# The first FFN product of a cross-attention block as seven block products instead of eight, with W1's parts streamed

## The chip, the cores and the metric

The kernel runs on one core of a Trainium2 chip. The metric is the device time of one execution in microseconds (us), lower is better.

## The reference

The input x has 8 batches of 1024 tokens with 512 channels, the context 8 times 64 rows of 384 channels. All is float32.

```python
x = x + xattn(layernorm(x), ctx_768, Wq, bq, Wk, bk, Wv, bv, Wo, bo)   # 16 heads of 32, 64 keys, softmax
h = layernorm(x) @ W1 + b1                                            # 512 -> 2048
imag = w_imag * sin(theta + 0.1 * h)
q = h + (cos(theta) * w_real + sin(theta) * w_imag) * imag * 0.1
x = x + relu(q) @ W2 + b2                                             # 2048 -> 512
```

The sine, the gate and the relu are elementwise on the hidden values h, of which there are 8192 x 2048.

## The kernel before

**Precision.** Each float32 product is made of three matmuls of 128x128 weights against 128x512 moving columns in the fp32r type: both operands are split into a high and a low part, and high x high, high x low and low x high are added up in PSUM (`product`, lines 1394 to 1396). The low part is the operand less its high part. So every operand of a product costs ScalarE (ACT) a copy to the high part and VectorE (DVE) or GpSimd (POOL) a subtraction for the low part.

**Stage A, attention.** 8192 tokens are 16 tiles of 512 (`TILES`), a tile has 4 blocks of 128 rows (`NB`), and 4 groups of heads make 64 steps. TensorE does queries, scores, transposes, values and output projection. Its result, x1, goes to DRAM (`x1_dram`). From the third tile on, the layer-normed rows are turned from token-major to channel-major without TensorE: DVE turns 32x32 squares (`turn_rows`), SyncE (SP) sends them to DRAM in four DMAs a half tile (`carry_out`) and reads them back in another order (`carry_back`).

**Stage B, FFN.** For each tile t and each chunk f of 128 of the 2048 hidden channels, TensorE makes the hidden values by 4 products of 3 matmuls (`xt_hi`/`xt_lo` against `w1a`/`w1b`), and then the second product of an earlier chunk, `second(j - LAG_B)`, 4 blocks of 3 matmuls. One chunk is 24 matmuls. W1 and W2 stay in SBUF in high and low parts. The other engines do, for each chunk: ACT `turns` (line 1010, from PSUM) and `hid` (1012, from PSUM); DVE `frac`, the rounding (1350); POOL turns less the rounding (820); ACT the sine (995); DVE `wave`, hid plus gain times sine (1320); ACT the relu to `act_hi` (1001); DVE `act_lo` (1325). For each tile there are also: POOL adds of the bias bo (637) and b2 (645), statistics (1049), the normalised rows (865), the turn of the rows through DRAM, and at the end DVE's addition of the four blocks of the second product (`residual`, 1313) and the store. Four hidden banks of PSUM rotate; `second` holds the other four for a whole tile.

Every engine runs its queue in the order written. Waits are on counting semaphores. SP issues nearly all DMAs, and it too waits in order.

**Between the stages.** At step 63 of stage A, SP loads x1 of tiles 0 and 1 (557, 558). Tile 0 is biased, normalised and turned by 16 transposes on TensorE (1400), right behind the last output projections. The first 8 chunks of W1 were split during stage A, one per tile (`split_hi`, `split_lo`).

## Time and profile before

| | us |
|---|---|
| median of three timed executions (2029.12 to 2029.51) | 2029.39 |
| span of the profiled execution (first to last instruction) | 2027.3 |
| first FFN matmul starts, us from the span's start | 630.33 |
| last matmul starts | 2023.53 |
| busy in the span: PE / DVE / ACT / POOL | 2014.9 / 1342.4 / 1131.6 / 1021.5 |

The profiled execution is one execution, and its own time is its span; a timed execution counts 2.1 us more. A busy PE says only that matmuls are in flight: a matmul is shown as 389 ns long while a new one starts about every 227 ns, so the pace is read from counts in a window. PEclk is the granted TensorE clock as a share of full speed; it reads 1.00 all through both stages.

### The profile page before, as it was taken

What the parts mean: (1) busy time and instruction counts of PE and PEld (TensorE: products, weight loads), DVE (VectorE), ACT (ScalarE), POOL (GpSimd) and SP (SyncE); (2) the same over time, 40 slices, a digit from 0 to 9 for tenths busy, and PEclk for the clock granted to TensorE, in tenths of its full rate; (3) what the DMA queues carried; (4) which work ended last, traced back from release to release, by engine and by line L of the source; (5) the groups of instructions that cost most, each with busy time, mean ns of one, the idle gap of its engine ahead of it and who ended that gap; (6) DMA issues with size and microseconds to landing.
All of it is one profiled execution on the core that took longest, in us unless ns stands there. A gap on an engine that the chain in (4) does not pass through costs nothing.

```text
span 2027.3 us, 26664 instructions
## 1 busy us (share of the span) xinstructions
PE 2014.9 (99%) x9498; PEld 1684.9 (83%) x9498; DVE 1342.4 (66%) x1983; ACT 1131.6 (56%) x1979; POOL 1021.5 (50%) x708
## 2 busy tenths in 40 slices
PE   9999999999999999999999999999999999999999
PEld 7788888888888888888888888888888888888887
DVE  8988888888876665655555555565655555555554
ACT  6767767667665655544554454545545454554453
POOL 6877777777774453435334343433435334343521
PEclk9999999999999999999999999999999999999999
DMA  7565675655524311121111212211130211112100
GB/s 240 150 164 136 169 175 138 173 137 164 143 66 144 107 42 42 45 81 27 57 42 42 54 40 73 42 42 42 42 83 21 64 43 42 46 48 73 42 22 21
DMA packets 232822, 168.51 MB, mean 83 GB/s; under 512 B 154353, under 2 KB 184049, under 8 KB 232689
## 3 DMA queue, kind: packets, MB, share of 16 engines
q1 hardware_dynamic: 231824, 166.76, 29.8%
q8 instruction: 75, 1.23, 0.3%
q14 instruction: 59, 0.48, 0.1%
q10 hardware_dynamic: 864, 0.04, 0.0%
HBM read 98.34 MB, written 68.16 MB: 82 GB/s over the span
## 4 chain that ended last, share of the span: by engine, by line
PE 91%; DVE 4%; ACT 2%; POOL 1%; issue 1%; DMA 1%; SPq 0%; ACTq 0%; DVEq 0%; POOLq 0%
PE psum L1394 29%; PE psum L1396 29%; PE psum L1395 29%; PE psum L1487 2%; DVE hid L1320 1%; POOL prob L679 0%; DVE act_lo L1325 0%; POOL prob L700 0%; ACT act_hi L1001 0%; ACT hid L1012 0%; DVE top L1177 0%; DVE prob L1168 0%; DMA x_sb<-in_x 0%; DVE xt_lo L1067 0%; DVE xt_lo L1277 0%
## 5 line engine op out<-in xcount | busy, mean ns | idle before, releaser
L820 POOL TENSOR_TENSOR frac<-turns,frac 128x512 f32<-128x512 f32 x256 | 333.3, 1302 | 826.9 <-DVE frac L1350 826.9
L1320 DVE SCALAR_TENSOR_TENSOR hid<-frac,gain,hid 128x512 f32<-128x512 f32 x256 | 321.7, 1257 | 144.2 <-ACT frac L995 143.1
L1394 PE MATMUL psum<-w_hi,act_hi 128*128 128x512 f32 x1024 | 398.3, 389 | 0.0
L1395 PE MATMUL psum<-w_lo,act_hi 128*128 128x512 f32 x1024 | 398.3, 389 | 0.0
L1396 PE MATMUL psum<-w_hi,act_lo 128*128 128x512 f32 x1024 | 398.3, 389 | 0.0
L1010 ACT ACTIVATE turns<-psum,u_shift 128x512 f32<-128x512 f32 x256 | 176.5, 689 | 328.4 <-PE psum L1396 271.2
L1001 ACT ACTIVATE act_hi<-hid 128x512 fp32r<-128x512 f32 x256 | 161.8, 632 | 353.9 <-DVE hid L1320 353.9
L1325 DVE SCALAR_TENSOR_TENSOR act_lo<-hid,act_hi 128x512 fp32r<-128x512 f32 x256 | 197.6, 772 | 178.1 <-ACT act_hi L1001 178.1
L1350 DVE TENSOR_SCALAR frac<-turns 128x512 f32<-128x512 f32 x256 | 111.4, 435 | 248.1 <-ACT turns L1010 248.1
L1395 PEld LDWEIGHTS psum<-w_lo,act_hi 128*128 128x128 f32 x1024 | 192.3, 188 | 40.0
L1394 PEld LDWEIGHTS psum<-w_hi,act_hi 128*128 128x128 f32 x1024 | 192.1, 188 | 39.9
L1396 PEld LDWEIGHTS psum<-w_hi,act_lo 128*128 128x128 f32 x1024 | 192.1, 188 | 39.8
L1394 PE MATMUL psum<-xt_hi,w1a_hi 128*128 128x512 f32 x512 | 199.5, 390 | 0.5 <-DVE xt_lo L1067 0.3
L1396 PE MATMUL psum<-xt_hi,w1a_lo 128*128 128x512 f32 x512 | 199.2, 389 | 0.0
L1395 PE MATMUL psum<-xt_lo,w1a_hi 128*128 128x512 f32 x512 | 199.2, 389 | 0.0
L1396 PE MATMUL psum<-xt_hi,w1b_lo 128*128 128x512 f32 x512 | 199.2, 389 | 0.0
L1394 PE MATMUL psum<-xt_hi,w1b_hi 128*128 128x512 f32 x512 | 199.2, 389 | 0.0
L1395 PE MATMUL psum<-xt_lo,w1b_hi 128*128 128x512 f32 x512 | 199.2, 389 | 0.0
L1012 ACT ACTIVATE hid<-psum,par 128x512 f32<-128x512 f32 x256 | 174.5, 682 | 0.0
L995 ACT ACTIVATE frac<-frac 128x512 f32<-128x512 f32 x256 | 161.4, 630 | 0.0
L700 POOL TENSOR_TENSOR prob<-prob,top 128x1024 f32<-128x1024 f32 x64 | 122.1, 1907 | 73.2 <-DVE top L1177 73.1
L679 POOL TENSOR_TENSOR prob<-prob,inv 128x1024 f32<-128x1024 f32 x64 | 123.6, 1931 | 42.1 <-DVE inv L1159 42.0
(149 smaller groups left out, 4013.1 us busy)
## 6 DMA issues: line engine op xcount, KB each, us to landing
res<-in_x SPq DMA_DIRECT2D x64, 256.0 KB, 3.8
x_dram<-res SPq DMA_DIRECT2D x64, 256.0 KB, 3.1
x_sb<-in_x SPq DMA_DIRECT2D x15, 1024.0 KB, 6.4
x_sb<-x_dram SPq DMA_DIRECT2D x15, 1024.0 KB, 5.5
xn<-turn_dram SPq DMA_DIRECT2D x30, 512.0 KB, 5.1
out<-x_sb SPq DMA_DIRECT2D x15, 1024.0 KB, 4.4
turn_dram<-kt SPq DMA_DIRECT2D x112, 128.0 KB, 2.4
x_sb<-turn_dram SPq DMA_DIRECT2D x28, 512.0 KB, 6.3
```

The costliest lines, as they stand in the source:

```text
L679: pool.tensor_tensor(rows, rows, inv[:, (i - 1) % 2, :].unsqueeze(2) .to_broadcast([P, NB * HG, KEYS]), ALU.mult).then_inc(prob_done, 1)
L700: pool.tensor_tensor(rows, rows, top[:, i % 2, :].unsqueeze(2).to_broadcast([P, NB * HG, KEYS]), ALU.subtract).then_inc(shift_done, 1)
L820: pool.tensor_tensor(frac[:, j % 2, :], turns[:, j % 2, :], frac[:, j % 2, :], ALU.subtract)\
L995: act.activation(frac[:, j % 2, :], frac[:, j % 2, :], ACT.Sin, scale=SIN_SCALE).then_inc(sin_done, 1)
L1001: act.activation(act_hi[:, j % ACTS, :], hid[:, j % 2, :], ACT.Relu).then_inc(act_hi_done, 1)
L1010: act.activation(turns[:, j % 2, :], hidden, ACT.Identity, bias=u_shift[:, f:f + 1], scale=0.1 / TWO_PI).then_inc(turns_done, 1)
L1012: act.activation(hid[:, j % 2, :], hidden, ACT.Identity, bias=par[:, 3, f:f + 1])\
L1320: dve.scalar_tensor_tensor(out=hid[:, j % 2, :], in0=frac[:, j % 2, :], scalar=gain[:, f:f + 1], in1=hid[:, j % 2, :], op0=ALU.mult, op1=A ...
L1325: dve.scalar_tensor_tensor(out=act_lo[:, j % ACTS, :], in0=hid[:, j % 2, :], scalar=0.0, in1=act_hi[:, j % ACTS, :].bitcast(F32), op0=ALU. ...
L1394: pe.matmul(o, a_hi, b_hi, start=first, stop=False)
L1395: pe.matmul(o, a_hi, b_lo, start=False, stop=False)
L1396: return pe.matmul(o, a_lo, b_hi, start=False, stop=last)
```

## The change

Two token tiles (512 tokens each) and two hidden chunks (128 channels each) form a 2x2 product, with the 512 input channels cut into two halves of 256. It is made by Strassen's scheme in Winograd's form: seven products of block sums where eight block products would do. The eight pairs of tiles (`FFN_PAIRS`) each run 8 steps p of two chunks. A step has seven products P1 to P7 of 6 matmuls each.

- **TensorE.** In the sweep over p it runs P1, P6, P4, P2, P5, P7, then (from p = 1) `second` of the two chunks of step p-1 for the pair's first tile, then P3. P2 is accumulated on top of P1 in bank 0, P7 on P6 in bank 1, P3 on P5 in bank 2, and P4 is alone in bank 3. After P1, a copy of it is taken (`keep_p1`) before P2 may start; after P6, `sum_u` before P7; after P5, `sum_v`, `hidden_21` and `hidden_22` before P3. After step 7 come the last two chunks of the first tile, and then a second sweep: `second` of all 16 chunks for the pair's second tile, whose hidden values wait in `late_hid`.
- **Operands of the pair.** Both tiles are turned through DRAM (also the first two; the 16 transposes at the start of stage B are gone), POOL makes four sums (`operand_sums`), and ACT and DVE make high and low parts of seven operands of 128x1024 (`operand_hi`, `operand_lo`).
- **W1.** During stage A, 28 jobs make the seven parts of W1 (POOL sums, ACT high parts, low parts on POOL and DVE in turn) and store them in DRAM. In stage B each product's part (256 KB) is loaded into a ring of 8.
- **W2.** It is split in the first pair's sweep (ACT and POOL), stored in DRAM, and then loaded for each chunk and tile (512 KB) into a ring of 4.
- **Hidden values.** In each step ACT adds a copy of P1, and DVE adds five sums with PSUM; `hid` from PSUM on ACT is left for one of the four blocks. Output sums go to a buffer of their own, `acc`, loaded from x1.
- **Bias.** POOL adds bo to tiles 2T+2 and 2T+3 in steps 0 and 1 of pair T, and the last bias to the two tiles of `acc` in steps 2 and 4, each as two instructions of 128x1024, ahead of the step's `fraction`s. The first two tiles' bo is added in stage A.

```diff
+PRODUCTS = ("P1", "P6", "P4", "P2", "P5", "P7", "P3")
+NP = len(PRODUCTS)
+OPERANDS = ("B11", "B21", "B22", "T1", "T2", "T4", "T3")
+MOVING = {"P1": "B11", "P2": "B21", "P3": "B22", "P4": "T4", "P5": "T1", "P6": "T2", "P7": "T3"}
+BANK_OF = {"P1": 0, "P2": 0, "P6": 1, "P7": 1, "P5": 2, "P3": 2, "P4": 3}
...
+        xo_hi = sbuf(pb, "xo_hi", [P, NP, 2, TOK], F32R)
+        xo_lo = sbuf(pb, "xo_lo", [P, NP, 2, TOK], F32R)
+        w1_ring = sbuf(pb, "w1_ring", [P, W1_SLOTS, 2, 2 * P], F32R)
+        temps = sbuf(pb, "temps", [P, 2, 2 * TOK])
+        p1_sb = sbuf(pb, "p1_sb", [P, TOK])
...
+        late_hid = sbuf(pb, "late_hid", [P, FC, TOK])
+        w2_ring = sbuf(pb, "w2_ring", [P, W2_SLOTS, 2, C], F32R)
+        acc = sbuf(pb, "acc", [P, 2, NB, C])
...
+        def events(T):
+            order = []
+            for p in range(FP):
+                i = T * FP + p
+                order += [("product", i, name) for name in PRODUCTS[:-1]]
+                if p:
+                    order += [("second", first_half(T, 2 * p - 2), None), ("second", first_half(T, 2 * p - 1), None)]
+                order.append(("product", i, PRODUCTS[-1]))
+            order += [("second", first_half(T, FC - 2), None), ("second", first_half(T, FC - 1), None)]
+            return order + [("second", second_half(T, c), None) for c in range(FC)]
         block = stack.enter_context(nc.Block())
...
+            def load_w1(n):
+                if n >= W1_SLOTS:
+                    sp.wait_ge(prod, n - W1_SLOTS + 1)
+                pair, m = divmod(n % (NP * FP), NP)
+                sp.dma_start(w1_ring[:, n % W1_SLOTS].bitcast(F32).rearrange("p s x -> p (s x)"), w1s[pair, m])\
+                    .then_inc(w1_in[n % W1_SLOTS], 16)
...
+            def load_w2(e):
+                c = e % FC
+                sp.wait_ge(f_psum, e - W2_SLOTS + 1)
+                sp.wait_ge(w2_stored[c % W2_SLOTS], 16 * (W1_JOBS // W1_OUTS + c // W2_SLOTS + 1))
+                sp.dma_start(w2_ring[:, e % W2_SLOTS].bitcast(F32).rearrange("p s x -> p (s x)"), w2s[c])\
+                    .then_inc(w2_in[e % W2_SLOTS], 16)
...
+            sp.wait_ge(q_psum, GROUPS)
+            for slot in range(W1_OUTS):
+                sp.wait_ge(w1_stored[slot], 16 * len(range(slot, W1_JOBS, W1_OUTS)))
+            for n in range(W1_SLOTS):
+                load_w1(n)
+            for c in range(STAGE):
+                load_w2_raw(c)
+            rows_back(1)
...
+                        for p, s, half in ((5, 0, 0), (6, 0, 1), (7, 1, 0)):
+                            if more and at == first_half(T, 2 * p - 1):
+                                rows_out(2 * T + 2 + s, half)
+                        if more and at == second_half(T, 1):
+                            rows_out(2 * T + 3, 1)
+                        if at == second_half(T, 1):
+                            store_acc(2 * T)
+                        if more and at == second_half(T, 3):
+                            rows_back(2 * T + 3)
+                            load_acc(2 * T + 2)
+                        if T + 2 < FFN_PAIRS and at == second_half(T, FC - 2):
+                            for s in range(2):
+                                load_rows(2 * T + 4 + s)
...
+                    if more and p < 2:
+                        for half in range(2):
+                            add_row_bias(2 * T + 2 + p, half)
...
+                    if p in (2, 4):
+                        for half in range(2):
+                            add_last_bias(2 * T + p // 4, half)
+                    for kind in range(3):
+                        fraction(4 * i + kind)
...
+                fraction(4 * (T * FP + FP) - 1)
+                if more:
+                    operand_sums(T + 1, ("T1", "T2", "T4", "T3"))
...
+            def keep_p1(i):
+                act.wait_ge(prod, at_prod(i, "P1"))
+                act.wait_ge(v_done, i)
+                act.activation(p1_sb[:], psum[:, BANK_OF["P1"], :], ACT.Copy).then_inc(p1_done, 1)
...
+            for T in range(FFN_PAIRS):
+                more = T + 1 < FFN_PAIRS
+                for p in range(FP):
+                    i = T * FP + p
+                    if p:
+                        sine(4 * i - 2)
+                        positive(first_half(T, 2 * p - 1))
+                        turn(i - 1, 3)
+                    keep_p1(i)
+                    if T == 0:
+                        w2_to_hi(2 * p)
+                        w2_to_hi(2 * p + 1)
+                    if p:
+                        sine(4 * i - 1)
+                    for at, s, half in ((4, 0, 0), (5, 0, 1), (6, 1, 0), (7, 1, 1)):
+                        if more and p == at:
+                            ffn_rows(2 * T + 2 + s, half)
+                    turn(i, 0)
+                    hidden(i)
+                    sine(4 * i)
+                    turn(i, 1)
+                    turn(i, 2)
+                    positive(first_half(T, 2 * p))
+                    sine(4 * i + 1)
...
+            def sum_u(i):
+                T, p = divmod(i, FP)
+                dve.wait_ge(prod, at_prod(i, "P6"))
+                dve.wait_ge(p1_done, i + 1)
+                if T:
+                    dve.wait_ge(act_lo_done, second_half(T - 1, 2 * p) + 1)
+                dve.scalar_tensor_tensor(out=late_hid[:, 2 * p, :], in0=psum[:, BANK_OF["P6"], :],
+                                         scalar=par[:, 3, 2 * p:2 * p + 1], in1=p1_sb[:], op0=ALU.add, op1=ALU.add)\
...
+            def hidden_22(i):
+                p = i % FP
+                dve.wait_ge(v_done, i + 1)
+                dve.wait_ge(c21_done, i + 1)
+                rows = late_hid[:, 2 * p + 1, :]
+                dve.tensor_tensor(rows, psum[:, BANK_OF["P5"], :], rows, ALU.add).then_inc(c22_done, 1)
...
+            for j in range(NP):
+                operand_lo(0, j)
+            dve.wait_ge(y_psum, TILES * NB)
+            dve.wait_ge(last_done, 1)
+            for T in range(FFN_PAIRS):
+                more = T + 1 < FFN_PAIRS
+                for p in range(FP):
+                    i = T * FP + p
+                    if p:
+                        wave(4 * i - 3)
+                        hidden_12(i - 1)
+                        whole(4 * i - 1)
+                        positive_lo(first_half(T, 2 * p - 1))
+                    sum_u(i)
+                    if p:
+                        wave(4 * i - 2)
+                        wave(4 * i - 1)
+                    whole(4 * i)
...
+                    if more and p == 7:
+                        turn_late_rows(2 * T + 3, 0)
+                    sum_v(i)
+                    hidden_21(i)
+                    hidden_22(i)
+                    wave(4 * i)
+                    whole(4 * i + 1)
+                    whole(4 * i + 2)
+                    positive_lo(first_half(T, 2 * p))
+                i = T * FP + FP
+                wave(4 * i - 3)
+                hidden_12(i - 1)
+                whole(4 * i - 1)
+                positive_lo(first_half(T, FC - 1))
+                wave(4 * i - 2)
+                positive_lo(second_half(T, 0))
+                add_outputs(2 * T)
+                positive_lo(second_half(T, 1))
+                wave(4 * i - 1)
+                if more:
+                    turn_late_rows(2 * T + 3, 1)
+                for c in range(FC):
+                    if c + 2 < FC:
+                        positive_lo(second_half(T, c + 2))
+                    if more and c in XT_AT:
...
+            def strassen(i, name):
+                p, n, j = i % FP, at_prod(i, name) - 1, OPERANDS.index(MOVING[name])
+                pe.wait_ge(w1_in[n % W1_SLOTS], 16 * (n // W1_SLOTS + 2))
+                if p == 0:
+                    pe.wait_ge(xo_lo_done, NP * (i // FP) + j + 1)
+                if name == "P1" and i:
+                    pe.wait_ge(hid_done, i)
+                elif name == "P6" and i:
+                    pe.wait_ge(v_done, i)
+                elif name == "P4" and i:
+                    pe.wait_ge(c21_done, i)
+                elif name == "P5" and i:
+                    pe.wait_ge(c12_done, i)
+                elif name == "P2":
+                    pe.wait_ge(p1_done, i + 1)
+                elif name == "P7":
+                    pe.wait_ge(u_done, i + 1)
+                elif name == "P3":
+                    pe.wait_ge(c22_done, i + 1)
+                w, to = w1_ring[:, n % W1_SLOTS], psum[:, BANK_OF[name], :]
+                for k in range(2):
+                    cols = slice(k * P, (k + 1) * P)
+                    m = product(to, (w[:, 0, cols], w[:, 1, cols]), (xo_hi[:, j, k, :], xo_lo[:, j, k, :]),
+                                name in OPENS and k == 0, k == 1, name not in OPENS)
+                m.then_inc(prod, 1)
...
-                    hi, lo = (w1a_hi, w1a_lo) if f < HALF1 else (w1b_hi, w1b_lo)
-                    for k in range(KC):
-                        if f == 0:
-                            pe.wait_ge(xt_lo_done, (TILES + t) * KC + k + 1)
-                        m = product(psum[:, f % NB, :], (hi[:, f % HALF1, k, :], lo[:, f % HALF1, k, :]),
-                                    (xt_hi[:, k, :], xt_lo[:, k, :]), k == 0, k == KC - 1)
-                    m.then_inc(h_psum, 1)
```

## Rows read from the trace of the kernel before

**Rows 1.** The page: busy time of each engine over the span

```profile
PE 2014.9 (99%) x9498; PEld 1684.9 (83%) x9498; DVE 1342.4 (66%) x1983; ACT 1131.6 (56%) x1979; POOL 1021.5 (50%) x708
```

**Rows 2.** Windows: stretch, length, busy us (count) of five engines, PEclk, DMA share, GB/s

```profile
500.00:600.00 100.00, 100.00 (x547) 86.54 (x547) 77.82 (x122) 65.30 (x126) 72.67 (x46) 1.00 0.43 115
1000.00:1500.00 500.00, 500.00 (x2208) 414.01 (x2207) 286.79 (x392) 251.29 (x415) 207.74 (x145) 1.00 0.18 47
```

**Rows 3.** Groups by line: busy us, mean ns | idle before, releaser

```profile
L820 POOL TENSOR_TENSOR frac<-turns,frac 128x512 f32<-128x512 f32 x256 | 333.3, 1302 | 826.9 <-DVE frac L1350 826.9
L1320 DVE SCALAR_TENSOR_TENSOR hid<-frac,gain,hid 128x512 f32<-128x512 f32 x256 | 321.7, 1257 | 144.2 <-ACT frac L995 143.1
L1325 DVE SCALAR_TENSOR_TENSOR act_lo<-hid,act_hi 128x512 fp32r<-128x512 f32 x256 | 197.6, 772 | 178.1 <-ACT act_hi L1001 178.1
L1010 ACT ACTIVATE turns<-psum,u_shift 128x512 f32<-128x512 f32 x256 | 176.5, 689 | 328.4 <-PE psum L1396 271.2 <-DVE act_lo L1325 56.6
L995 ACT ACTIVATE frac<-frac 128x512 f32<-128x512 f32 x256 | 161.4, 630 | 0.0
L679 POOL TENSOR_TENSOR prob<-prob,inv 128x1024 f32<-128x1024 f32 x64 | 123.6, 1931 | 42.1 <-DVE inv L1159 42.0
L1350 DVE TENSOR_SCALAR frac<-turns 128x512 f32<-128x512 f32 x256 | 111.4, 435 | 248.1 <-ACT turns L1010 248.1
...
L1313 DVE TENSOR_TENSOR x_sb<-psum,x_sb 128x512 f32<-128x512 f32 x64 | 39.9, 682 | 2.4 <-PE psum L1396 2.4
```

**Rows 4.** Timeline, four places: start us, length, engine, line

```profile
616.31 1.29 POOL L637 TENSOR_TENSOR x_sb<-x_sb,bo_row 128x512 f32<-128x512 f32 x1 [2.91 <-DMA x_sb<-x_dram]
...
676.63 0.74 DVE L1320 SCALAR_TENSOR_TENSOR hid<-frac,gain,hid 128x512 f32<-128x512 f32 x1
676.79 1.74 POOL L820 TENSOR_TENSOR frac<-turns,frac 128x512 f32<-128x512 f32 x1 [6.01 <-DVE frac L1350]
...
1511.69 1.28 POOL L820 TENSOR_TENSOR frac<-turns,frac 128x512 f32<-128x512 f32 x1 [4.74 <-DVE frac L1350]
1511.70 1.83 DVE L1320 SCALAR_TENSOR_TENSOR hid<-frac,gain,hid 128x512 f32<-128x512 f32 x1
```

**Rows 5.** DMA issues: count, KB each, median us from issue to landing

```profile
out<-x_sb SPq DMA_DIRECT2D x15, 1024.0 KB, 4.4
turn_dram<-kt SPq DMA_DIRECT2D x112, 128.0 KB, 2.4
x_sb<-turn_dram SPq DMA_DIRECT2D x28, 512.0 KB, 6.3
```

**Rows 6.** Windows: a turned tile read back, and an x1 tile loaded; last two columns

```profile
1486.00:1488.00 2.00, 2.00 (x11) 1.65 (x10) 1.21 (x2) 1.18 (x3) 1.29 (x1) 1.00 1.02 214
...
1518.00:1520.00 2.00, 2.00 (x10) 1.65 (x10) 0.79 (x2) 1.03 (x2) 0.00 (x0) 1.00 1.04 404
```

**Rows 7.** Timeline of the passage from stage A to stage B

```profile
615.51 0.43 SPq L558 DMA_DIRECT2D x_sb<-x_dram  x1
...
620.64 2.47 DVE L1049 BATCH_NORM_STATS2 stats<-x_sb 128x6 f32<-128x512 f32 x4
...
623.81 1.02 POOL L616 TENSOR_TENSOR rstd<-var_eps,minus_half 128x4 f32<-128x4 f32 x1 [2.06 <-DVE var_eps L1056]
...
625.06 2.93 ACT L865 ACTIVATE xn<-x_sb,shift_rows,rstd 128x512 f32<-128x512 f32 x4 [5.58 <-DVE shift_rows L1061]
...
627.70 0.39 PE L1396 MATMUL psum<-wo_hi,o_lo 128*128 128x512 f32 x1
...
630.33 0.47 PE L1394 MATMUL psum<-xt_hi,w1a_hi 128*128 128x512 f32 x1 [0.26 <-DVE xt_lo L1067]
```

**Rows 8.** TensorE at the start, a turn of squares, and the last matmul

```profile
3.03 8.90 PE L1436 MATMUL psum<-kbd 128*128 128x512 f32 x30 [3.03 <-DVE kbd L1094]
...
675.17 1.24 DVE L1379 STREAM_TRANSPOSE turned_early<-xn 128x1024 f32<-128x1024 f32 x1
...
2023.53 0.39 PE L1396 MATMUL psum<-w_hi,act_lo 128*128 128x512 f32 x1
```

895 lines of the change are left out of this document (549 added, 346 removed).

## The prediction

> **What bounds the kernel now.** I read the busy times of the page first: TensorE has work in flight for 2014.9 of 2027.3 us, no other engine for more than 1342.4 [rows 1]. Then the windows, for the pace. Stage B issues 2208 matmuls in 500 us, 226.5 ns each, at a granted clock of 1.00 (the upper level, 2.4 GHz) and with nothing between them. VectorE is busy 287, ScalarE 251 and GpSimd 208 of those 500 us [rows 2]. The groups by line say why those engines aren't busier: nearly all their idle time ends on one another, in a ring turns, rounding, fraction, sine, wave, relu, low part, and this ring starts when TensorE delivers a chunk [rows 3]. So time goes by the count of matmuls, and the question for the change is whether the ring still fits beside a shorter TensorE stream, and what happens where TensorE's stream is cut.
>
> **The matmuls taken out: -87.0 us.** Before, a pair of tiles and two chunks take 2 x 2 x 12 = 48 matmuls of the first product; after, 7 x 6 = 42. That is 6 x 64 = 384 fewer, x 0.2265 = 87.0 us. FFN matmuls go from 6144 (1391.6 us; measured 630.33 to 2023.76, that is 1393.4 [rows 7, 8]) to 5760, 1304.6 us. A step of the sweep becomes 66 matmuls, 14.95 us; step 0 has no `second` and is 9.5 us.
>
> **The passage between the stages: +37.5 us.** Before, the last output projection ends at 627.9 and the first FFN product starts at 630.3 [rows 7]. After, P6 needs operand T2, which needs both tiles turned through DRAM. I follow that chain on the clock of before.
> VectorE begins statistics at 620.6 and does both tiles (2 x 3.1), so the shift of tile 0 comes at 627.0 and that of tile 1 after its GpSimd step at 628.1. ScalarE normalises at 0.73 a block: 628.6, 630.1, 631.5, 633.0. VectorE turns the first two halves by 631.4 (1.24 each, [rows 8]).
> SP sends half 0 at 630.2 to 632.2 and half 1 by 634.2 (four issues; one takes 0.43 [rows 7], I count 0.5), they land 2.4 after issue, and SP reads them back at 634.6 and 636.1; landing takes 6.3 [rows 5], so 640.9 and 642.4. The same DRAM buffer then takes tile 1: out 640.9 to 644.9. Before it is read back, SP issues 8 loads of W1 parts and 2 of W2, some 0.4 us each: the read goes out at 649.5 and, behind 2.6 MB of loads, lands at about 658.
> GpSimd forms T1 and T2 (2 x 2.5, below), the high and low part take 1.2 each: P6 at about 667. T4's low part waits behind GpSimd's next sum, so P4 starts at 670.6, which in an undisturbed step is 2.7 us after its beginning. The step thus begins in effect at 667.9, against 630.3. Bounds: +25 (both round trips at the 5 us of an unqueued read, sums at 1.3) to +48.
> TensorE stands still for some 18 us twice here. At the start of the kernel, after a standstill, 30 matmuls of this size take 8.9 us, 297 ns each [rows 8], against 6.8 at the usual pace. I add that 2.1 us once. The trace's clock shows 1.00 there, so it does not say why. The Trainium skill (TensorE: Matmul & The Clock Gate, What's actually happening) says that an idle array falls to 1.2 GHz and is back at 2.4 GHz once it has been busy; no row of this trace shows a fall inside the run, and the sum goes by the row.
>
> **The wait before P3 of step 0: +18 us.** With no `second` before it, P3 waits for P7 through `sum_v`, `hidden_21`, `hidden_22`. P7 ends at 8.15, is visible 0.2 later, and three VectorE operations with PSUM, 0.68 each [rows 3], end at 10.4. 2.25 us in each of 8 pairs. In other steps the two `second` hide it (P3 starts at 13.6).
>
> **The ring in the sweep: +23 us.** Per step VectorE has 4 waves, 5 sums, 4 roundings, 2 low parts: in pure work 4 x 0.74 + 5 x 0.68 + 4 x 0.44 + 2 x 0.77 = 9.7 us [rows 3, 4], and 1.2 for statistics and turns (8 of 0.62 and 4 of 1.24 over 8 steps [rows 7, 8]). But a wave reads two SBUF tensors, and beside GpSimd's operation it is held: both started at 1511.7, GpSimd took 1.28, the wave 1.83 = 1.28 + 0.55; when the wave came first (676.63), GpSimd took 1.74 instead of 1.29 [rows 4]. So they go one at a time.
> The Trainium skill (SBUF — State Buffer, Who interferes with whom) says that the one that starts first keeps the port for its whole instruction. The rows show it for 1.3 us instructions only; by the rule the new ones of 128x1024 hold VectorE twice as long.
> A plain step by hand, from P1 = 0: P2 done 5.6, turns 6.3, rounding 6.8, fraction 8.2, sine 8.8; h21 and h22 9.7 and 10.4; wave 11.1; fractions 12.9 and 14.7; wave of the second chunk 15.25; `hidden_12` 15.9; relu and turns on ScalarE 16.7; `keep_p1` of the next step 17.35. P2 needs it at 14.95 + 4.08 = 19.0: 1.7 us to spare.
> With two bias instructions ahead of the step's first fraction the ring gets longer than the step. A block of 512 takes 1.29 undisturbed [rows 4], so 1024 takes 2.55; the row of that size, with one operand broadcast, is 1.93 [rows 3]. I take 2.2, and 0.45 each time VectorE's turn is let in: 5.3 us a step, a ring of some 15.9 against 14.95. At 1.93 it is 15.2, at 2.55 with every wave held 16.6. The spare 1.7 goes in the first such step. From step 0 (only 9.5 + 2.25 long) into step 1 TensorE waits 1.3 us before P2; into steps 2 and 3, 0.9 each; step 3 has no bias and recovers; step 4 just fits. 3.1 us x 7, and 1.3 in the last pair, which has fewer adds. Bounds 8 (1.93) and 40 (2.55).
> The first pair also splits W2: GpSimd 2 x 1.3 more a step, ScalarE 2 x 0.63. On a step with bias that adds about 2.6: +8 us (3 to 12).
>
> **The DMA queue in the second sweep: +17.5 us.** SP's transfers share one queue. When chunk 1 of that sweep is done (5.4 us in) SP issues a W2 part (0.52 MB), half a turned tile (0.52), the store of 1.05 MB (4.4 us when alone [rows 5]); then two W2 parts, the turned tile back (1.05), the load of acc (1.05) and a fourth W2 part, which chunk 8 needs at 21.8. At 404 GB/s, and 214 for the turned tile [rows 6], that is 5.2 + 1.3 + 2.6 + 2.6 us at 404, 4.9 for the tile read back, and, by my estimate from the slower of the two rates, 1.2 more for the half tile: 17.8 us of transfer. It starts at 6.7, since a transfer starts over 1 us after its issue, and lands at 25.2. TensorE waits 3.4 us if the queue is strictly in order, nothing if transfers overlap. I take 2.5, x 7 pairs.
>
> **The attention stage: +3 us.** GpSimd gets 14 low parts (2.2 each) and 16 sums (1.3), VectorE 14 low parts less 8 old ones. GpSimd is busy 72.7 and VectorE 77.8 of 100 us there [rows 2], and these stand at ends of steps; I take 3 of 0 to 10. W1's part loads (256 KB for each 1.36 us product, 193 GB/s against 404) come seven products ahead and stay hidden, as do W2's in the first sweep.
>
> **Sum.** -87.0 + 37.5 + 2.1 + 18 + 23 + 8 + 17.5 + 3 = +22.1. Span 2027.3 -> 2049.4; a timed run counts 2.1 more, so 2051.
>
> **Rivals.** (1) *Faster: the ring stays inside the step.* Place: GpSimd's bias adds in steps 0 to 2. If a 1024 add goes at the 1.93 of the attention rows or faster and the waves slip in between, the 23 shrinks to 2 and the first pair's 8 to 1: 2023. For it: such a row exists, and TensorE waits nowhere now. Against: the add of two real rows has 1.29 for 512. The point at which it decides: one-off costs are 37.5 + 2.1 + 8 + 3 = 50.6, so 36.4 us are left for 8 pairs, 4.55 each; P3's wait takes 2.25, so ring and DMA together must stay under 2.3 us a pair. I have 5.3. (2) *Slower still: the lock decides.* Adds of 2.55 that hold each wave to their end, DMA strictly in order: ring 40 and DMA 24, passage 42, first pair 12: 2083. (3) *The DMA queue costs nothing* because transfers overlap: 2033. For it: the load share reads above 1.00 at places; against: shares near 1.00 are full engines. (4) *The passage is much shorter*, 20 us instead of 37.5: 2033. Against: each round trip is three SP waits in order.
>
> **How the numbers follow.** Forecast, with every term near its middle, 0.42; rival 1 and what is like it 0.25, of which 0.02 ends within 0.2%; rival 2, 0.15; rivals 3 and 4, 0.18, of which 0.05 faster and 0.03 within 0.2%. A measurement of this kernel tells about 0.2% (4 us) from no change. Faster 0.28, same 0.05, slower 0.67. The likeliest case's own range is 2036 to 2066. The range for 8 in 10 takes in most of rivals 1 and 2: 2010 to 2078.
>
> **What would show it.** In the profile after: 9098 matmuls; first FFN matmul about 648, the second product only about 667; windows inside stage B where TensorE has 2208 a 500 us in plain steps; a wait of TensorE for VectorE's `hidden_22` of 2.2 us eight times; waits for ScalarE's `p1_sb` of about 1 us in steps 1 to 3 and none in 5 to 7; one wait for `w2_ring` of about 3 us in seven pairs. The forecast fails if the passage is much under 37 us, or if the waits for `p1_sb` and `w2_ring` are absent or are several us in every step.

## The result and the profile after

The changed kernel takes 2200.07 us (median of 4 runs, 2199.49 to 2202.72) against 2029.26 beside it (4 runs, 2029.07 to 2029.51): ratio 1.0845, 95% interval 1.0830 to 1.0861. I had forecast slower, 2051 with a range to 2078. The side was right, the size was not: 171 us in place of 22.

The page of the kernel after, busy time of each engine, beside [rows 1]; then the granted clock; then the windows of [rows 2]:

```profile
PE 1995.6 (91%) x9098; PEld 1628.4 (74%) x9098; DVE 1711.0 (78%) x2279; ACT 1095.1 (50%) x1855; POOL 1192.7 (54%) x728
```

```profile
core 0: 2197.5 us, clock 0.971
```

```profile
500.00:600.00 100.00, 95.92 (x517) 81.10 (x517) 84.27 (x131) 65.04 (x125) 77.72 (x51) 1.00 0.65 181
1000.00:1500.00 500.00, 460.11 (x1958) 371.40 (x1957) 383.48 (x463) 221.49 (x342) 221.52 (x121) 0.98 0.74 235
```

The 400 matmuls less are there (9098). But 500 us of stage B hold 1958 where 2208 stood, and the 100 us of the attention stage 517 where 547 stood. VectorE went from 287 to 383 of 500 us.

I split the difference of the spans, 170.2 us, at four places: the last output projection (it ends 0.23 us after its last start), P4 of the first pair (2.7 us behind the step's start in effect), the starts of the pairs, and the end. The matmuls of the first two places, by timeline:

```profile
672.36 0.39 PE L1805 MATMUL psum<-wo_hi,o_lo 128*128 128x512 f32 x1
...
717.47 0.76 PE L1803 MATMUL psum<-xo_hi,w_ring 128*128 128x512 f32 x1 [19.30 <-DVE xo_lo L1649]
718.03 0.63 PE L1804 MATMUL psum<-xo_lo,w_ring 128*128 128x512 f32 x1
...
720.77 0.76 PE L1803 MATMUL psum<-xo_hi,w_ring 128*128 128x512 f32 x1 [0.40 <-DVE xo_lo L1649]
```

Pairs are counted from 0, as steps are.

| part | forecast | measured |
|---|---|---|
| 384 matmuls | -87.0 | -87.0 |
| attention stage (last projection 627.9 -> 672.6) | +3 | +44.7 |
| passage, with its slow clock (720.77 - 2.7 - 672.6 - 2.4) | +39.6 | +43.0 |
| first pair from there, over its 163.1 us of matmuls | +15.9 | +35.5 |
| pairs 1 to 6 over theirs | +47.1 | +130.2 |
| pair 7 | +3.6 | +5.3 |
| stalls of stage B that before already had | | -1.8 |
| sum | +22 | +170 |

So 42 us of the error lie in the attention stage, 83 in pairs 1 to 6, 20 in the first pair. Pair 7, which prepares nothing for a next pair, is nearly as forecast. That is the first hint: what costs is not the seven products.

What TensorE waited for, over the whole span (us in total, times, longest). L1684 is `hidden_22`, for which P3 waits; `p_sb` is the copy of P1, for which P2 waits; then come the W2 ring and the two waits of the passage.

```profile
PE psum L1803 <- DVE late_hid L1684: 41.0, 26, 2.5
PE psum L1803 <- ACT p_sb L1272: 34.5, 29, 6.0
PE psum L1803 <- DMA w_ring<-w2s: 32.1, 9, 5.5
PE psum L1803 <- DMA w_ring<-w1s: 22.5, 1, 22.5
PE psum L1803 <- DVE xo_lo L1649: 19.7, 2, 19.3
```

By step, the mean of pairs 1 to 6: steps 0 to 7 take 13.3, 17.8, 18.4, 16.1, 15.7, 16.2, 15.0 and 15.0 us, where matmuls alone are 9.5 and seven times 14.95. In pair 7 steps 1 to 7 take 15.4, 15.0, 15.1, 15.0, 15.1, 15.0 and 15.0.

The page's rows of the elementwise operations, beside [rows 3]: the rounding went from 435 to 680 ns, the fraction from 1302 to 1518.

```profile
L1053 POOL TENSOR_TENSOR frac<-turns,frac 128x512 f32<-128x512 f32 x256 | 386.7, 1518 | 452.9 <-DVE frac L1697 452.9
...
L1697 DVE TENSOR_SCALAR frac<-turns 128x512 f32<-128x512 f32 x256 | 169.8, 680 | 104.7 <-ACT turns L1290 103.0
...
L1707 DVE SCALAR_TENSOR_TENSOR late_hid<-frac,gain,late_hid 128x512 f32<-128x512 f32 x128 | 168.2, 1314 | 8.5 <-ACT frac L1303 5.3
```

The timeline shows why, in step 1 of pair 3 (VectorE and GpSimd alone):

```profile
1305.14 5.66 POOL L789 TENSOR_TENSOR x_sb<-x_sb,bo_row 128x1024 f32<-128x1024 f32 x2
...
1305.88 2.65 DVE L1707 SCALAR_TENSOR_TENSOR late_hid<-frac,gain,late_hid 128x512 f32<-128x512 f32 x1 [0.15 <-ACT frac L1303]
...
1308.46 2.62 DVE L1697 TENSOR_SCALAR frac<-turns 128x512 f32<-128x512 f32 x1
...
1311.16 1.29 POOL L1053 TENSOR_TENSOR frac<-turns,frac 128x512 f32<-128x512 f32 x1 [0.37 <-DVE frac L1697]
```

Two adds of the bias run back to back on GpSimd; from 1000 to 1500 us they are these two groups, with the fraction:

```profile
L1053 POOL TENSOR_TENSOR frac<-turns,frac 128x512 f32<-128x512 f32 x84 | 127.1, 1521 | 144.7 <-DVE frac L1697 144.7
L789 POOL TENSOR_TENSOR x_sb<-x_sb,bo_row 128x1024 f32<-128x1024 f32 x12 | 31.7, 2658 | 61.3 <-DMA x_sb<-x_dram 61.3
L800 POOL TENSOR_TENSOR acc<-acc,b_row 128x1024 f32<-128x1024 f32 x8 | 22.6, 2846 | 0.0
```

VectorE's wave, 0.74 us when alone [rows 4], ends 0.55 us behind the first of them (at 1308.54, the add at 1307.99), and the rounding behind it, 0.43 alone, 0.28 behind the second. The next fraction waits for that rounding and starts at 1311.16. I had let the wave be held; the rounding, which has one input in SBUF, I had at its 0.44. The Trainium skill (SBUF — State Buffer, Who interferes with whom) lists `tensor_scalar` among the operations that can enter the two-port modes and so be held by GpSimd for a whole instruction. This trace agrees in that the rounding is held, for 2.62 us; which mode it ran in, it does not show.

The adds are held too. Over the whole span their lengths are (min/median/max ns):

```profile
L789 POOL TENSOR_TENSOR x_sb<-x_sb,bo_row x28: 2352/2563/2866, 727.7 to 1863.2; 128x1024 f32<-128x1024 f32 x28
L800 POOL TENSOR_TENSOR acc<-acc,b_row x32: 2407/2844/2857, 765.2 to 2091.2; 128x1024 f32<-128x1024 f32 x32
```

From 1000 to 1500 us an add takes 2.39 or 2.40 us where no operation of VectorE was under way at its start, 2.83 to 2.86 behind a wave that was, and 2.54 to 2.56 behind a held rounding.

### The profile page after: what moved, and what is told of

Read it like the earlier page. It is cut to its first block, busy times and chain, and to the rows that moved or that the text cites. A ratio compares the mean times of both kernels' runs of the same rounds, so it can differ in the third digit from the quotient of the medians.

```text
span 2197.5 us, 27862 instructions
## 1 busy us (share of the span) xinstructions
PE 1995.6 (91%) x9098; PEld 1628.4 (74%) x9098; DVE 1711.0 (78%) x2279; ACT 1095.1 (50%) x1855; POOL 1192.7 (54%) x728
## 4 chain that ended last, share of the span: by engine, by line
POOL 24%; DVE 24%; PE 22%; issue 12%; ACT 10%; DMA 6%; SPq 3%; DVEq 0%; POOLq 0%; ACTq 0%
POOL frac L1053 11%; PE psum L1803 7%; PE psum L1804 7%; PE psum L1805 7%; DVE frac L1697 5%; DMA w_ring<-w2s 3%; POOL prob L882 3%; ACT turns L1290 3%; DVE prob L1506 2%; DVE top L1515 2%; DVE xt_lo L1617 2%; ACT frac L1303 2%; DMA x_sb<-x_dram 2%; POOL halves L869 2%; POOL q_lo L782 2%
## 5 line engine op out<-in xcount | busy, mean ns | idle before, releaser
L1803 PE MATMUL psum<-xo_hi,w_ring 128*128 128x512 f32 x896 | 363.6, 406 | 117.9 <-DVE late_hid L1684 41.0
L1803 PE MATMUL psum<-w_ring,act_hi 128*128 128x512 f32 x1024 | 406.2, 397 | 41.3 <-DMA w_ring<-w2s 32.1
L1804 PE MATMUL psum<-w_ring,act_hi 128*128 128x512 f32 x1024 | 402.8, 393 | 0.0
L1805 PE MATMUL psum<-w_ring,act_lo 128*128 128x512 f32 x1024 | 402.7, 393 | 0.0
L1804 PE MATMUL psum<-xo_lo,w_ring 128*128 128x512 f32 x896 | 357.4, 399 | 0.0
L1805 PE MATMUL psum<-xo_hi,w_ring 128*128 128x512 f32 x896 | 357.1, 399 | 0.0
L1803 PEld LDWEIGHTS psum<-xo_hi,w_ring 128*128 128x128 f32 x896 | 173.4, 194 | 177.4 <-issue 142.6
L1803 PEld LDWEIGHTS psum<-w_ring,act_hi 128*128 128x128 f32 x1024 | 195.3, 191 | 91.6 <-DMA w_ring<-w2s 35.9
L1805 PEld LDWEIGHTS psum<-w_ring,act_lo 128*128 128x128 f32 x1024 | 194.7, 190 | 41.5
L1804 PEld LDWEIGHTS psum<-w_ring,act_hi 128*128 128x128 f32 x1024 | 195.3, 191 | 39.9
L1805 PEld LDWEIGHTS psum<-xo_hi,w_ring 128*128 128x128 f32 x896 | 173.2, 193 | 37.8
L1804 PEld LDWEIGHTS psum<-xo_lo,w_ring 128*128 128x128 f32 x896 | 174.0, 194 | 35.1
L1707 DVE SCALAR_TENSOR_TENSOR late_hid<-frac,gain,late_hid 128x512 f32<-128x512 f32 x128 | 168.2, 1314 | 8.5 <-ACT frac L1303 5.3
L1707 DVE SCALAR_TENSOR_TENSOR hid<-frac,gain,hid 128x512 f32<-128x512 f32 x128 | 149.3, 1167 | 25.3 <-ACT frac L1303 21.9
```

What stands on the lines that cost most here:

```text
L1707: dve.scalar_tensor_tensor(out=rows, in0=frac[:, q % 2, :], scalar=gain[:, f:f + 1], in1=rows, op0=ALU.mult, op1=ALU.add).then_inc(wave_do ...
L1803: pe.matmul(o, a_hi, b_hi, start=first, stop=False, skip_group_check=resumed)
L1804: pe.matmul(o, a_hi, b_lo, start=False, stop=False, skip_group_check=resumed)
L1805: return pe.matmul(o, a_lo, b_hi, start=False, stop=last, skip_group_check=resumed)
```

## The experiments

Times stand beside 2200.07 of the kernel after. Each experiment but the last was executed once, and four executions of the kernel after lie 3.2 us apart; spans and the positions in them are from one profile each. "Pair" is the mean of pairs 1 to 6, 184.8 us after, "sweep" its sweep, 127.4 after, 114.1 of it matmuls.

**att_no_jobs.** In `hi_of_job`, `lo_of_job` and `sum_of_blocks`:

```diff
+                w = 2 * P if J < W1_OUTS else 1
-                act.activation(w1_out[:, J % W1_OUTS, :, 0, :], quad_part(r), ACT.Copy).then_inc(w1_hi_done, 1)
+                act.activation(w1_out[:, J % W1_OUTS, :, 0, 0:w], quad_part(r)[:, :, 0:w], ACT.Copy).then_inc(w1_hi_done, 1)
```

> The splits and sums of W1 in the attention stage are done in full for the first four jobs and the first quad only and on one column of each row after that (the other W1 parts in DRAM are then stale values); all transfers, waits and semaphores stay. Theory A (the jobs' work on ScalarE, VectorE and GpSimd lies on the critical ring of the attention steps): the last output projection, at 669.9 us in the kernel after and 625.2 in the kernel before, comes at 633 to 640, and the span is 2160 to 2168. Theory B (the delay comes from the transfers of the jobs and from the early bias rows): it stays at 660 or later and the span above 2185.

2181.67 us, span 2179.9. The last projection:

```profile
647.89 0.39 PE L1808 MATMUL psum<-wo_hi,o_lo 128*128 128x512 f32 x1
```

That is 24.5 us earlier than in the kernel after. Counted by its first matmul it comes at 645.4, between the 633 to 640 of theory A and the 660 of B: the work of the jobs is the larger part of the delay, but not all that A gave it. The span falls by 17.6 us only, between A and B as well: the passage and the first pair keep the gain to 1 us, pairs 1 to 6 take 185.8 us each in place of 184.8. No run says whether that difference is more than chance.

**att_no_early_bias.** The two calls of `bias_early_row` and VectorE's wait for `res_biased` are gone.

> The output bias of the first rows is not added on GpSimd in the attention stage, and VectorE does not wait for it. Theory A (GpSimd's wait for the row that the bias is added to holds the next steps by 7 to 8 us, once): the last output projection comes at 661 to 663 instead of 669.9, and the span is 2189 to 2192. Theory B (that wait is only where a delay of the ring shows, and the steps behind it would lose the time anyway): less than 3 us.

2187.66 us, span 2185.9 (11.7 less); the last projection 14.2 us earlier, more than A's 7 to 9. The place in the kernel after:

```profile
88.36 1.26 POOL L808 TENSOR_TENSOR res<-res,bo_row 128x512 f32<-128x512 f32 x1 [7.09 <-DMA res<-in_x]
```

GpSimd waited 7.09 us for a load, and behind it in its order stood `q_lo`, for which TensorE then waited. In the waits of TensorE from 60 to 640 us this is the 7.8 (kernel after), and 8.2 where the jobs are gone, so the jobs have no part in it:

```profile
PE psum L1803 <- POOL q_lo L782: 15.0, 11, 7.8
```

```profile
PE psum L1806 <- POOL q_lo L783: 11.3, 5, 8.2
```

**early_row_end.** `bias_early_row(0)` moves from ahead of GpSimd's work on `prob` to the end of the same step.

> The bias of the first output row is added by GpSimd at the end of its seventh attention step, not at its start, so that what follows in its order does not wait for the load of that row. Without any early bias the last output projection came 14.2 us earlier, 7.8 of them by step 8. Theory A (the first of these is the wait for the load): the projection of step 8 is at 101 to 103 instead of 109.3, the last one 6 to 8 us earlier and the span 2190 to 2192. Theory B (the wait only moves to VectorE, which adds this row's product): less than 3 us.

2195.62 us. The projection of step 8 comes at 102.8, the last one 6.6 us earlier (665.75 against 672.36). Theory A; only the span, 2193.6, lies above its 2190 to 2192.

**att_no_sums.** Only the sums of W1's blocks are cut, the splits stay.

> Only GpSimd's sums of W1 blocks (four for each quad, 1.52 us each) are cut to one column after the first quad; the splits on ScalarE, VectorE and GpSimd stay in full. With all of the preparation cut, the last output projection came 24.3 us earlier than in the kernel after. Theory A (GpSimd's 12 sums and 14 low parts, some 36 us of work, carry this): 10 to 14 us earlier. Theory B (VectorE's and ScalarE's splits carry it): less than 4 us.

2188.64 us; the last projection 14.1 us earlier:

```profile
658.26 0.39 PE L1806 MATMUL psum<-wo_hi,o_lo 128*128 128x512 f32 x1
```

12 sums of 1.52 us are 18.3 us of GpSimd, and TensorE got 14.1 back. By difference the splits of 24 jobs are the other 10.4. Theory A, at its upper end.

**att_neither.** Both of the first two edits.

> The W1 preparation in the attention stage cut to one column after the first four jobs, and no early bias rows. Alone they brought the last output projection 24.3 and 14.2 us earlier than in the kernel after, which has it 44.7 us later than the kernel before. Theory A (two separate additions to the same ring): together 38 to 40 us, so it comes at 630 to 632 of 625.2 before, and the jobs and sums of the first quad that are still there are the rest. Theory B (each is partly hidden behind the other): they give more together, 43 us or over, or less than 32.

```profile
634.44 0.39 PE L1802 MATMUL psum<-wo_hi,o_lo 128*128 128x512 f32 x1
```

2163.60 us, 36.5 less. The last projection is 37.9 us earlier, 24.5 and 14.2 are 38.7: they add up, at the lower edge of A's 38 to 40. 6.7 us of 44.7 remain; four jobs and the first four sums are still done here and, at the rate of the others (24.5 / 24 jobs), account for 4 of them.

**ffn_no_bias.** In `add_row_bias` and `add_last_bias`:

```diff
-                pool.tensor_tensor(rows, rows, bo_row[:].unsqueeze(1).to_broadcast([P, NB // 2, C]), ALU.add)\
+                pool.tensor_tensor(rows[:, :, 0:1], rows[:, :, 0:1],
+                                   bo_row[:, 0:1].unsqueeze(1).to_broadcast([P, NB // 2, 1]), ALU.add)\
```

> Both bias adds on GpSimd in the FFN stage are cut to one column of each row (outputs lack the biases); waits stay. Theory A (the bias adds of 2.6 to 2.8 us stand ahead of the fractions in GpSimd's order, and this makes the sweep's steps longer than 15 us): the sweep of pairs 1 to 6 falls from 127.4 us to 118 to 121, the span by 45 to 60 us, to 2137 to 2152. Theory B (the ring through VectorE and ScalarE sets the steps, and GpSimd's adds are beside it): the span falls by less than 15 us.

2127.60 us, 72.5 less: more than theory A's upper end. The sweep is 118.6 us; its steps 2 to 7 take 15.0 each, the bare 66 matmuls. The first pair loses 13.4 us less. The rounding, by its line (min/median/max ns), in the kernel after and here, from 1000 to 1500 us:

```profile
L1697 DVE TENSOR_SCALAR frac<-turns x84: 418/427/2622, 1003.0 to 1499.0; 128x512 f32<-128x512 f32 x84
```

```profile
L1699 DVE TENSOR_SCALAR frac<-turns x90: 419/422/429, 1003.7 to 1496.4; 128x512 f32<-128x512 f32 x90
```

The medians agree; what made the mean 680 were single ones that were held: 45 of all 256 took over 0.6 us, 20 of them over 2.

**ffn_no_row_bias.** The same cut for `add_row_bias` alone.

> Of GpSimd's bias adds in the FFN stage only those of the next pair's rows (four of 2.6 us in the first two steps of a pair) are cut to one column of each row; the adds of the last bias (four of 2.8 us, steps 2 and 4) stay in full. With both cut, the sweep of pairs 1 to 6 fell from 127.4 to 118.6 us. Theory A (each pair of adds costs in its own step, by the time that it stands ahead of a fraction): steps 1 and 2 lose their 3 us each, steps 3 and 5 keep their 1.2, the sweep is 121 to 122 us and the span falls by 40 to 48 us. Theory B (the last-bias adds, at 2.8 us each, carry the loss as well): the span falls by 25 to 35 us. In both, pair 7, which has no row bias, stays at 168.4 us.

2165.33 us, 34.7 less. The sweep is 122.3: step 1 falls from 17.8 to 16.1 and step 2 from 18.4 to 15.6, steps 3 and 5 keep 16.15; but the span falls by 34, not 40 to 48, because the last-bias adds carry the other 37.7 of the 71.7 that its span fell without both. So B is right on the sum. 22.7 of the 37.7 stand in the sweeps of pairs 1 to 6 and 6 in the first pair; the rest is in second sweeps, which differ by some 1 us a pair between single profiles. I had charged steps 4 to 7 nothing.

The same run says something that I had overlooked. Pair 7 has the same last-bias adds in steps 2 and 4, but no next pair to prepare (statistics, normalised rows, turns). There steps 3, 4 and 5 take 15.1, 15.0 and 15.1; in pairs 1 to 6 they take 16.15, 15.7 and 16.15. And without any adds (ffn_no_bias) the steps with the preparation take 15.0. So neither the adds nor the preparation costs much alone: together they are too much for the ring. No run moves the adds behind a step's fractions, or takes the preparation out, to say which part of it matters.

**one_add_a_step.** The eight adds of a pair stand one in each step.

```diff
-                    if more and p < 2:
-                        for half in range(2):
-                            add_row_bias(2 * T + 2 + p, half)
+                    if more and p < 4:
+                        add_row_bias(2 * T + 2 + p // 2, p % 2)
...
-                    if p in (2, 4):
-                        for half in range(2):
-                            add_last_bias(2 * T + p // 4, half)
+                    if p >= 4:
+                        add_last_bias(2 * T + p // 2 - 2, p % 2)
```

> The same sums as after: GpSimd's eight bias adds of a pair (four for the next rows, four for the last bias) are spread at one for each step, where before two stood one behind the other in steps 0, 1, 2 and 4. GpSimd's total work is unchanged. Theory A (two adds, 5.3 to 5.7 us, are more than the gap between the fourth fraction of a step and the first of the next; one of 2.7 us fits): the sweep of pairs 1 to 6 comes to 118.6 to 121 us, the span falls by 50 to 72 us, to 2126 to 2148. Theory B (GpSimd's share of the SBUF port, taken by its adds from VectorE's operations, costs the time, wherever they stand): the span falls by less than 20 us.

2192.84 us, 7 less, and the sweep is 125.3, not 118.6 to 121. Theory A, that it is the queue of two adds, falls. The timeline of this kernel shows what one add does (two waves in one row):

```profile
1349.10 3.95 DVE L1705 SCALAR_TENSOR_TENSOR late_hid<-frac,gain,late_hid 128x512 f32<-128x512 f32 x2
...
1349.63 2.86 POOL L800 TENSOR_TENSOR acc<-acc,b_row 128x1024 f32<-128x1024 f32 x1
```

Two waves take 2.02 where no add runs (next kernel); here they take 3.95: VectorE again waits an add out, and the steps that had been clean (6 and 7) now are 15.8 and 16.2.

**bias_on_vector.** The same adds on VectorE, as sixteen blocks of 512 a pair.

```diff
+            def bias_piece(T, p, n):
+                if 1 <= p <= 4 and T + 1 < FFN_PAIRS:
+                    add_row_bias(2 * T + 2 + (p - 1) // 2, 2 * ((p - 1) % 2) + n)
+                elif p >= 5:
+                    add_last_bias(2 * T + (p - 5) // 2, 2 * ((p - 5) % 2) + n)
...
+                    bias_piece(T, p, 0)
                     whole(4 * i)
+                    bias_piece(T, p, 1)
```

> The same sums as after, but the sixteen blocks of bias of a pair are added on VectorE, 512 elements at a time (two in each of steps 1 to 7 and two in the second sweep), and GpSimd keeps the fractions and the operand sums. Spreading the adds over GpSimd's steps had left the loss where it was. Theory A (GpSimd's adds lengthen VectorE's two-operand operations and the rounding that run at the same time, over their shared path to SBUF): the rounding goes back from 665 to some 430 ns and the wave operation of late_hid from 1302 to under 1050, and as the adds on VectorE take some 0.7 us each the sweep of pairs 1 to 6 is 118.6 to 122 us; the span falls by 40 to 72 us, to 2126 to 2158. Theory B (the adds' work itself is too much for the ring, whichever engine has it): the span falls by less than 20 us or grows.

2169.75 us, 30.3 less. The rounding is at 422 ns at most 431, the wave of `late_hid` at 983, one add takes 0.69:

```profile
1289.35 2.02 DVE L1721 SCALAR_TENSOR_TENSOR late_hid<-frac,gain,late_hid 128x512 f32<-128x512 f32 x2
...
1291.29 0.69 DVE L1367 TENSOR_TENSOR x_sb<-x_sb,bo_row 128x512 f32<-128x512 f32 x1
```

Steps 1 to 3 of a pair are clean now (15.0 to 15.2), steps 4 to 7 take 15.8 to 16.5; the sweep is 123.2 and the span's gain is below what A named. So both hold a part: the hold on VectorE is gone, and 0.69 us twice a step is still too much where ScalarE's normalised rows and VectorE's turns stand in the same steps. In pair 7, which has adds in steps 5 to 7 and neither of those, these steps take 15.0. (Adds and the update of b2's row stand at other places in the order as well.)

**w2_split_small.** From the fifth chunk on the splits of W2 in the first pair are cut to one column.

> In the first pair the splits of W2 on ScalarE and GpSimd are cut to one column from the fifth chunk on (W2 in DRAM is then partly stale); waits and transfers stay. The forecast charged 8 us for these splits. Theory A (they carry what the first pair loses beside the passage and beyond the other pairs, some 16 us): the first pair, 221.4 us, comes to 205 to 209. Theory B (half of it is the passage and the late start of the ring): to 212 to 215, the span falls by 6 to 9 us.

2191.78 us, 8.3 less; the first pair 214.0 against 221.4. Theory B: 12 of 16 chunks cost what my term of 8 us had for all; the splits of the first four are still done here.

**rows_back_first.** `rows_back(1)` moves ahead of the loads of W1 parts and of W2.

> The load of the second tile's turned rows is issued ahead of the eight W1 loads and the first W2 loads in SyncE's order; nothing else is changed. Theory A (of the 19.7 us that the first P6 waits, 8 W1 loads and the raw W2 loads stand ahead of the turned rows in the queues for 3 to 8 us): the first FFN product does not come earlier, P6 waits 12 to 17 us, and the span falls by 3 to 8 us. Theory B (GpSimd's and VectorE's operand chain sets that wait, and the rows are there in time): within 1 us.

2195.58 us, 4.5 less. The passage of this kernel, TensorE's waits:

```profile
700.75 0.77 PE L1803 MATMUL psum<-xo_hi,w_ring 128*128 128x512 f32 x1 [28.37 <-DMA w_ring<-w1s]
710.59 0.77 PE L1803 MATMUL psum<-xo_hi,w_ring 128*128 128x512 f32 x1 [6.94 <-DVE xo_lo L1649]
```

P6 waits 12.4 us less, but the first W1 part lands 5.5 us later. So the queue's order costs some 7 us of the passage, of which 4.5 reach the time, and the rest is the chain itself. Theory A, with a shorter wait of P6 (6.9) than its 12 to 17.

**acc_load_later.** The residual rows' load moves from step 3 to step 9 of the second sweep.

> The 1 MB load of the next pair's residual rows is issued in step 9 of the second sweep, not in step 3, where it stands right behind the store of the first output tile and the last turned rows. Theory A (what the second sweep waits for is the W2 ring behind these three large transfers in the queues): the one wait for W2, 4.2 to 6.2 us in each of pairs 0 to 6, falls below 2.5 us, and the span by 12 to 25 us. Theory B (the wait is the price of the store and of the turned rows alone, which come first): less than 5 us, or the wait comes again further on.

2197.85 us: no change that a single run can tell. The wait for W2 does fall, to 0.9 to 1.8, as A has it; but three chunks further on a wait of 2.7 to 2.9 for `act_lo` comes in each pair. The turned rows land when they did, ScalarE stands at them in its order for 5.3 us, and the relu of the next chunk stands behind. So B's last clause holds: the wait comes again further on.

**rows_back_later.** The turned rows' load too, from step 3 to 5.

> In the second sweep SyncE issues the load of the last turned rows in step 5 (before: step 3, two steps behind their store), and the residual rows' load in step 9. Moving the latter alone had changed nothing. Theory A (SyncE stands at this load until the store has landed, 3 to 5 us, with the loads for the W2 ring behind it): the one wait for W2 of pairs 0 to 6, 4.2 to 6.2 us, falls below 1.5 us and the slow-clock matmuls behind it with it; the span falls by 25 to 50 us. Theory B (the bytes of the store and of the turned rows in the queues cause it): less than 8 us. A rival cost: the operands of the next pair come later, and its first products wait.

2210.92 us, 10.9 more. In this kernel's waits of TensorE from 1000 to 1500 us the one for W2 has gone (but for one of 0.7), and the one for `act_lo` has grown:

```profile
PE psum L1804 <- DVE act_lo L1715: 21.6, 9, 4.5
```

ScalarE and VectorE stood in their order at operands whose rows had not come, with the relu and the low part of the next chunk behind them: the rival cost, inside the sweep. SyncE's timelines, first after, then here:

```profile
1241.85 2.05 SPq L561 DMA_DIRECT2D turn_dram<-temps  x4
...
1247.24 5.34 SPq L568 DMA_DIRECT2D x_sb<-turn_dram  x2
1252.63 2.18 SPq L687 DMA_DIRECT2D acc<-x_dram  x1
1255.22 19.73 SPq L672 DMA_DIRECT2D w_ring<-w2s  x8
```

```profile
1246.53 1.86 SPq L561 DMA_DIRECT2D turn_dram<-temps  x4
...
1257.37 4.21 SPq L568 DMA_DIRECT2D x_sb<-turn_dram  x2
```

The two read-backs keep SyncE for 5.34 us, and even when issued 9 us after the stores for 4.21. So it isn't the landing of the store that it waits for, as I had argued; the issue itself takes that long here (4.5 us for the second of the two, and 3.6 in the later case), and W2's loads stand behind it. Why it does, no run shows.

**operands_later.** As before, and `XT_AT = (1, 2, 9, 10, 11, 12, 13)` in place of `(1, 2, 7, 8, 9, 10, 11)`.

> As the run before with the turned rows' load in step 5 and the residual rows' in step 9 of the second sweep, and the next pair's last five operand splits on ScalarE and VectorE two steps later as well (steps 9 to 13, before: 7 to 11). In that run the wait for the W2 ring had gone and one for act_lo of 6 us had come, because ScalarE and VectorE stood in their order at operands whose rows had not landed. Theory A (with the splits moved too, neither wait is left): the second sweep of pairs 0 to 6, 49.3 to 52.3 us in the kernel after, comes to 44 to 45.5, and the span falls by 30 to 45 us. Theory B (the chain of rows, sums and splits is as long as what is left of the sweep, so it shows again, at the next pair's first products or in the sweep): the span falls by less than 10 us.

2175.30 us, 24.8 less. The second sweep is 46.2 to 47.9 in place of 49.2 to 52.3, and TensorE's wait for W2 is gone but for 0.5 to 1.1 us in three pairs. A wait for `act_lo` of 1.2 to 2.6 is left in each, so neither theory is met: A had 44 to 45.5 and 30 to 45 us, B less than 10.

**all_moves.** The four edits that leave the results as they are: `bias_on_vector`, `early_row_end`, `rows_back_first` and `operands_later`.

> Four edits that leave every result as it is, together: the biases of the FFN stage on VectorE (31 us off the span alone), the first early bias row at the end of its step (4 us), the second tile's turned rows ahead of the first W1 loads (4 us), and the later loads and splits in the second sweep (0 to 45 us). Theory A (the losses lie one behind the other in time, and add up): 2200 less 39 and less what the second sweep gives, 2116 to 2161, so 4 to 6.5 per cent above the kernel before. Theory B (one fixed loss only uncovers the next): above 2165.

2131.68 us (4 runs, 2129.40 to 2133.99) against 2028.85: ratio 1.0512, interval 1.0494 to 1.0529. The single gains are 30.3 + 4.5 + 4.5 + 24.8 = 64.1, together they give 68.4: they add up, and theory A holds. It is the best version here and still 5% slower than the kernel before.

## Why the prediction was wrong

- **Matmuls, -87.0:** right.
- **Attention, +3: failed.** The step was "these stand at ends of steps; I take 3 of 0 to 10". GpSimd was busy 72.7 of 100 us [rows 2], and I took the rest for room. But the added work did stand in TensorE's way: 12 of the 16 sums and 24 of the 28 jobs cost TensorE 24.5 us, and rows of early bias, which I did not charge at all, 14.2, of which half is one wait for a load put ahead of `q_lo` in GpSimd's order. The stage measured 44.7 longer.
- **Passage, +37.5 and +2.1 for the clock:** measured 43.0. The chain that I followed was the right one; the clock was cheap in the forecast (below).
- **Wait before P3 of step 0, 2.25 us a pair:** measured 2.45 and, with the slow matmuls behind it, 3.8 (13.3 us against 9.5). "In other steps the two `second` hide it" failed: in pairs 1 to 6 P3 waits 1.2 us in step 1, 1.8 in step 2 and 0.5 in step 4 as well. These are waits of the ring; without bias adds they are gone.
- **Ring in the sweep, +23, bounds 8 to 40: the main term mis-sized.** The place (GpSimd's bias adds) was right: without them steps 2 to 7 take 15.0 us. But they cost 72 us, more than three times the term and nearly twice its upper bound. For steps 1 to 5 of a pair I had losses of 1.3, 0.9, 0.9, 0 and 0 us; measured are 2.8, 3.5, 1.2, 0.7 and 1.2. The length of the adds is not what failed: 2.4 when nothing of VectorE was under way before them, 0.45 more behind a wave, two in line 5.66 where I had 5.3. Two other things are. First, VectorE stood until an add's end, 2.65 and 2.62 us in a row; I had let the wave be held and not the rounding. Second, the plain step has none of the 1.2 us a step of statistics and turns that I had counted just before, nor ScalarE's normalised rows. "Step 3 has no bias and recovers; step 4 just fits" comes nearly true in pair 7, which prepares nothing, and fails in all others, where the last-bias adds of steps 2 and 4 carry 37.7 us. How the 72 us divide between the two no run shows (bias_on_vector, which ends the hold, gets 30.3 back); one_add_a_step shows that it isn't a matter of two adds in line.
- **First pair's W2 split, +8:** 7.4 to 8.3 for 12 of the 16 chunks. The other 12 us by which that pair missed are adds of bias (13.4 us there in all) and slow matmuls.
- **DMA in the second sweep, +17.5, 2.5 a pair: mis-sized.** The wait is there, once a pair as said (two pairs have a second short one), with 3.9 to 5.5 us. With slow matmuls the second sweep lost 5.7 to 8.8, 47 us in all. The sum by bytes missed that SyncE needs 5.3 us to issue the two read-backs, and that ScalarE and VectorE stand at these rows with the next chunks behind them. (17.8 us of transfer from 6.7 on end at 24.5, not at 25.2.)
- **Rivals.** Rival 2, the lock decides, was the nearest (ring 40), and still too cheap. Rival 1's ring is what the seven products do by themselves: without bias adds no step of pairs 1 to 6 but step 0 has a wait in the sweep. In its arithmetic ring and DMA come to 5.1 us a pair, not 5.3.
- **Signs.** Nearly all that I named came: 9098 matmuls, eight waits for `hidden_22`, waits for the copy of P1 of 0.3 to 1.2 us in steps 1 to 3, one for W2 in seven pairs. In step 5, where I had said none, such a wait came with 0.9. The two start times, 648 and 667, came 47 and 50 us late, nearly all of it the attention stage's, and none of my conditions for a failed forecast looked at that stage.

## What to carry to other kernels

In a pipeline whose engines wait for one another in a ring, idle time of an engine is not all room. The last-bias adds cost a step 0 to 0.2 us where nothing else was added (pair 7) and 0.7 to 1.2 where the next tiles were prepared too, and an add on GpSimd can hold an operation of VectorE until it ends, whether two adds stand in line or one in each step. Before helpers are hung on the freed time of such a change, add up all of them in one step by hand, price each as if it were on the path, look for one that waits for a load ahead of work that others need, and count what its DMA issues hold behind them. Here 87 us of matmuls were bought with 45 us in the attention stage, 43 in the passage, 72 of adds, 47 in the second sweeps and about 30 before P3 of step 0 (each rounded; with 8 for the splits of W2 this leaves some 15 of the 171 us unassigned).

## What the hardware showed that I had not expected

The granted clock falls inside the run after short standstills. TensorE's timeline at the wait for W2 in pair 2, kernel after, and the windows there (clock in the third column from the end):

```profile
1257.34 0.39 PE L1805 MATMUL psum<-w_ring,act_lo 128*128 128x512 f32 x1
1262.08 0.80 PE L1803 MATMUL psum<-w_ring,act_hi 128*128 128x512 f32 x1 [4.36 <-DMA w_ring<-w2s]
1262.67 0.63 PE L1804 MATMUL psum<-w_ring,act_hi 128*128 128x512 f32 x1
1263.10 0.63 PE L1805 MATMUL psum<-w_ring,act_lo 128*128 128x512 f32 x1
```

```profile
1260.00:1262.00 2.00, 0.00 (x0) 0.00 (x0) 2.00 (x2) 1.54 (x2) 1.99 (x1) 0.89 1.02 410
1262.00:1264.00 2.00, 1.92 (x5) 1.53 (x6) 2.00 (x2) 0.74 (x1) 1.92 (x2) 0.50 1.03 412
1264.00:1266.00 2.00, 2.00 (x8) 1.63 (x7) 2.00 (x1) 0.32 (x1) 2.00 (x1) 0.76 0.28 111
```

After 4.36 us of standstill the clock is at 0.50, the lower level of 1.2 GHz, and matmuls start 0.43 us apart, not 0.227; after six of them it is up again. The wait of 2.45 us before P3 of step 0 does the same (matmuls at 1296.65 to 1298.36 start 0.43 apart). The waits of 1.8 us before P3 of step 2 have no such fall behind them (the clock is 1.00 there). The Trainium skill (TensorE: Matmul & The Clock Gate, What's actually happening) says that an idle array falls to 1.2 GHz and is back at 2.4 GHz once it has been busy; this trace agrees. The forecast named that rule and went by the rows of before, which showed no such fall. Summed over stage B, the starts of matmuls that no idle time stands before lie 44 us further apart than 0.2265 each (12.5 in the first pair, 4.3 to 6.2 in pairs 1 to 6, 2.4 in pair 7), where the kernel before has 1.4; all_moves, with fewer waits, has 28 and a mean clock of 0.985. I had charged 2.1. A wait of this length thus costs more than itself. How much of the 44 is the clock alone no run here separates.
